# Three attention stages and two feed-forward stages of a transformer kernel merged into one sequence of 24 batches with a guest in the slots

## What is computed

```python
x = x + L0_attn(layernorm(x))   # block mask: 16 heads of 8, scores outside the allowed blocks are 0, biases
x = x + L0_ffn(layernorm(x))    # FP4: (silu(xq @ Wg) * (xq @ Wu)) quantised again, @ Wd; hidden 352
x = x + L1_attn(layernorm(x))   # causal mask with ALiBi bias
x = x + L1_ffn(layernorm(x))    # ternary: silu(w1) * w2, then two square 512x512 layers with gelu, w3
x = x + L2_attn(layernorm(x))   # full softmax, no output projection
x = x + L2_ffn(layernorm(x))    # RWKV
x = x + L3_attn(layernorm(x))   # state-space block
x = x + L3_ffn(layernorm(x))    # eight low-rank experts
```

## Time and profile before

| what | value |
|---|---|
| median of three runs | 2219.01 us (2218.09 to 2221.08) |
| profiled execution, span from first to last instruction | 2215.5 us |
| instructions | 34423 |
| busy PE, DVE, ACT, POOL | 1867.7, 1282.6, 1049.3, 712.8 us |
| mean granted TensorE clock | 0.921 |

### The profile page before, as it was taken

The page is one execution under the profiler, slowest core; times in us unless marked ns, Lnnn a source line. Parts: engine busy times, 40 slices in busy tenths (PEclk is TensorE's granted clock), DMA queues, the critical chain, the costliest instruction groups (busy, mean ns, idle before and its releaser), DMA issues.

```text
span 2215.5 us, 34423 instructions
## 1 busy us (share of the span) xinstructions
PE 1867.7 (84%) x12909; PEld 864.2 (39%) x12909; DVE 1282.6 (58%) x2930; ACT 1049.3 (47%) x1768; POOL 712.8 (32%) x796
## 2 busy tenths in 40 slices
PE   2788788756569989998999999899999967999998
PEld 0233233224344555554444444333333324444443
DVE  1666666637767666673110111489989916776663
ACT  1266565532123655565222222188888854445432
POOL 3176666545532322220110011122233115443330
PEclk9799999867868999998899999799999978999999
DMA  8323343000023343220000002143223110000000
GB/s 195 66 58 67 71 87 65 1 11 1 1 57 59 68 89 77 59 59 2 2 0 1 0 1 57 26 89 60 59 58 81 36 48 1 1 10 5 6 5 15
DMA packets 70270, 91.58 MB, mean 41 GB/s; under 512 B 13228, under 2 KB 63772, under 8 KB 65228
## 3 DMA queue, kind: packets, MB, share of 16 engines
q1 hardware_dynamic: 64536, 84.42, 18.5%
q10 hardware_dynamic: 5568, 4.96, 0.7%
HBM read 49.10 MB, written 39.85 MB: 40 GB/s over the span
## 4 chain that ended last, share of the span: by engine, by line
PE 52%; issue 5%; DVE 5%; ACT 4%; DMA 2%; SPq 1%; POOL 1%; DVEq 0%; POOLq 0%; ACTq 0%
PE ps L1401 9%; PE ps L417 5%; DVE mx L685 3%; PE ps L2798 3%; PE ps L391 3%; PE ps L375 3%; PE ps L2078 2%; PE ps L403 2%; PE ps L2080 2%; PE ps L2096 2%; PE ps L353 2%; PE ps L330 2%; PE ps L1391 2%; DMA Qst<-mT 1%; PE ps L1771 1%
## 5 line engine op out<-in xcount | busy, mean ns | idle before, releaser
L685 DVE TENSOR_REDUCE mx<-ps 128x1 f32<-128x512 f32 (+3 forms) x1536 | 755.8, 549 | 255.8 <-PE ps L353 121.4
L593 ACT ACTIVATE Pr<-ps 128x1024 f32<-128x1024 f32 (+3 forms) x512 | 350.1, 705 | 233.0 <-PE ps L335 117.4
L586 ACT ACTIVATE Pr<-ps 128x512 f32<-128x512 f32 x512 | 274.6, 600 | 48.4 <-PE ps L391 43.1
L353 PE MATMUL ps<-Kst,Qst 63*128 63x512 bf16 (+3 forms) x1024 | 235.2, 326 | 60.8 <-DVE mx L685 38.2
L330 PE MATMUL ps<-Qst,Kst 64*128 64x512 bf16 (+3 forms) x1024 | 229.2, 324 | 48.6 <-issue 32.1
L375 PE MATMUL ps<-Pr,V 128*32 128x512 f32 (+3 forms) x2048 | 204.5, 473 | 4.4 <-ACT ctxU L599 3.1
L403 PE MATMUL ps<-Kst,Qst 63*128 63x512 bf16 x512 | 169.3, 401 | 6.6 <-DVE mx L685 4.4
L417 PE MATMUL ps<-Pr,V 128*32 128x256 f32 x2048 | 165.1, 394 | 8.4 <-ACT ctxU L599 7.5
L2826 POOL TENSOR_TENSOR ve<-mv,eps 128x4 f32<-128x4 f32 x41 | 8.8, 214 | 502.4 <-DVE mv L2815 502.4
L391 PE MATMUL ps<-Qst,Kst 64*128 64x512 bf16 x512 | 154.4, 388 | 14.9 <-issue 9.0
L1509 DVE SCALAR_TENSOR_TENSOR f_shared<-ps,w_L_s_w,f_own 128x512 f32<-128x512 f32 x32 | 23.4, 748 | 230.6 <-ACT f_own L1462 199.6
(11 more groups left out here) (342 smaller groups left out, 3355.5 us busy)
## 6 DMA issues: line engine op xcount, KB each, us to landing
Qst<-parts_scratch SPq DMA_DIRECT2D x48, 384.0 KB, 6.0
Kst<-parts_scratch SPq DMA_DIRECT2D x48, 384.0 KB, 8.4
parts_scratch<-qpart SPq DMA_DIRECT2D x48, 192.0 KB, 2.7
parts_scratch<-kpart SPq DMA_DIRECT2D x48, 192.0 KB, 2.7
parts_scratch<-qpart SPq DMA_DIRECT2D x48, 128.0 KB, 2.6
parts_scratch<-kpart SPq DMA_DIRECT2D x48, 128.0 KB, 2.7
parts_scratch<-qpart SPq DMA_DIRECT2D x48, 64.0 KB, 2.3
parts_scratch<-kpart SPq DMA_DIRECT2D x48, 64.0 KB, 2.3
```

Of the source, the lines that this page charges most:

```text
L353: mm = pe.matmul(ps[:, 4 + a, lo:lo + W], k.Qst[rows, n.par, pair, P * it:P * it + P], k.Kst[rows, n.par, pair, 0:W], start=True, stop=not ...
L586: act.activation(k.Pr[:, g % 2, 2 * (j // 2) + 1 - j % 2, :], ps[:, self.bank_t(b, g, j), :], ACT.Exp).then_inc(self.s_exp.sem, 1)
L593: act.activation(k.Pr[:, g % 2, 2 * tile:2 * tile + 2, 0:W], ps[:, 2 * tile:2 * tile + 2, 0:W], ACT.Exp).then_inc(self.s_exp.sem, 1)
L685: dve.tensor_reduce(k.mx[:, half, at:at + 1], ps[:, bank, lo:lo + W], AX_X, ALU.max, negate=True).then_inc(self.s_max.sem, 1)
```

## The change

The stages `Attention`, `Fp4Ffn`, `Attention`, `TernaryFfn`, `Attention` become one object `Run` with 26 frames (numbers -1 to 24), whose frame F holds batch F of a sequence of 24: eight of the block, eight of the alibi, eight of the full attention. There is no wait for a whole stage any more until the tail. A feed-forward is a guest of the frames: `Fp4Ffn` in frames 2 to 10 (its first half for batch F-2, its second half for batch F-3), `TernaryFfn` in frames 11 to 19 (the same, with F-11 and F-12). Its matmuls stand in three places of a slot, between the attention's own. From frame 20 on there is no guest.

PSUM is divided anew: banks 0 and 1 transposed scores, 2 and 3 scores for the maxima, 4 and 5 guest, 6 context, 7 the rest. So a tile of transposed scores has one pair of banks where it had two. The two heads of a tile are issued next to each other, and one DVE reduction reads both heads. In the full attention each kind takes turns in two banks up to frame 19 and in three from frame 20.

The guest's own work changes: ACT's silu and gelu read and write SBUF in one instruction over all columns (1408 for FP4, 2048 for ternary), after DVE (ternary) or ACT (FP4) has copied the products out of PSUM; each needs a table load before it and one after it for the exponentials. The square layers are computed bank by bank. The block attention's power of minus one on POOL becomes a reciprocal on DVE (`dve_recip`). The norm of a guest has tiles of its own.

```diff
-        frames(pe, frame)
...
+class Run:
+    FRAMES = range(-1, 3 * NB + 1)
+    LONE = 20
...
+    def guests(self, F):
+        fp4, ternary = self.ffns
+        out = []
+        if F <= NB + 2:
+            out.append(fp4)
+        if F >= ternary.FIRST - 1:
+            out.append(ternary)
+        return out
...
+    def pe_quarter(self, pe, F, s, part, b, g, pb, pg, mb, c):
+        hosting = F < self.LONE
+        t, tn = self.of(b)
+        if t:
+            if t.kind == "full":
+                t.pe_head_t(pe, tn, g, part, hosting)
+            elif part % 2 == 0:
+                t.pe_scores_t(pe, tn, g, part // 2)
+        if part in (0, 2):
+            self.pe_guest(pe, F, s, part)
+        m, mn = self.of(mb)
+        if m:
+            if m.kind == "full":
+                m.pe_head_m(pe, mn, c, part, hosting)
+            elif part % 2 == 0:
+                m.pe_scores_m(pe, mn, c, part // 2)
+        p, pn = self.of(pb)
+        if p and p.kind == "full" and part % 2:
+            p.pe_context(pe, pn, pg, part // 2, 2)
+        elif p and p.kind != "full" and part == 3:
+            p.pe_context(pe, pn, pg, 0, 1)
+        if part == 1:
+            self.pe_guest(pe, F, s, part)
+            self.pe_out(pe, F, s)
...
+    def act_exps(self, act, F, s, b, g):
...
+            t.act_exps(act, tn, g, 0)
+        self.act_guest(act, F, s, 0)
+        if t:
+            t.act_exps(act, tn, g, 1)
...
-            out = ps[:, 2 * tile + a, 0:W]
...
+    def pe_scores_t(self, pe, b, g, tile):
+        pe.wait_ge(self.s_exp.sem, self.s_exp.at(b, 2 * g + tile))
...
+        for a in (1, 0):
+            rows = slice(64 * a, 64 * a + 64)
+            mm = pe.matmul(ps[:, PAIR_T + a, 0:W], k.Kst[rows, b.par, 2 * q + tile, P * jt:P * jt + P],
+                           k.Qst[rows, b.par, 2 * q + tile, T - W:T], start=True, stop=not tri)
...
-                    dve.tensor_reduce(k.mx[:, half, at:at + 1], ps[:, bank, lo:lo + W], AX_X,
+            dve.tensor_reduce(heads[:, :, 4 * i + it:4 * i + it + 1], k.ps[:, PAIR_M:PAIR_M + 2, lo:lo + W], AX_X,
+                              ALU.max, negate=True).then_inc(self.s_max.sem, 2)
...
+    def bank_t(self, b, g, j, hosting):
+        t = 64 * b.c + 4 * g + j
+        return PAIR_T + t % 2 if hosting else t % 3
...
-            pool.tensor_tensor(k.rec[:, :, :], k.dn2[:, :, :],
-                               k.mone[:, 0:1].unsqueeze(2).broadcast_to([P, NT, 4]), ALU.pow)                .then_inc(self.s_part.sem, 1)
+        dve.reciprocal(k.rec[:, :, :], k.dn2[:, :, :]).then_inc(self.s_recip.sem, 1)
...
-class TernaryFfn(Stage):
+class TernaryFfn(Ffn):
+    UNITS = ((("turn",), ("h2", 0, 0), ("h2", 0, 1)),
+             (("h2", 0, 2), ("h2", 0, 3), ("gate", 0)),
...
+    FIRST = 11
+    SILU, GELU_B, GELU_A = 3, 9, 14
...
-                act.activation(dst[:, m, :], ps[:, src + m, :], ACT.Gelu, scale=scale[:, m:m + 1])\
-                   .then_inc(done.sem, 1)
+            act.activation(self.h, self.h, ACT.Silu).then_inc(self.s_gate.sem, 1)
...
+            act.activation(self.a, self.a, ACT.Gelu).then_inc(self.s_a.sem, 1)
...
+    def dve_first(self, dve, n, j):
+        dve.tensor_scalar(self.a[:, j, :], self.k.ps[:, self.bank(self.H1 + j), :], self.sh1[:, j:j + 1], None,
+                          ALU.mult).then_inc(self.s_a_raw.sem, 1)
```

More of the change, by code:

```diff
@@ L45, in valid @@
     def valid(self):
[L46 to L51 removed]
+        return 0 <= self.c < NB
 class Signal:
@@ new lines, in pe_scores_m @@
+    def pe_scores_m(self, pe, n, c, r):
+        k, ps = self.k, self.k.ps
+        pair, rounds = self.rounds(c)
+        if r >= len(rounds):
+            return
+        u, its = rounds[r]
+        if u == 0:
+            pe.wait_ge(self.s_stacked.sem, self.s_stacked.at(n))
+        pe.wait_ge(self.s_max.sem, self.s_max.at(n, u))
+        tri = self.kind == "alibi"
+        for it in its:
+            W, lo = self.span(it), self.place(its, it)
+            for a in range(2):
+                rows = slice(64 * a, 64 * a + MROW)
+                mm = pe.matmul(ps[:, PAIR_M + a, lo:lo + W], k.Qst[rows, n.par, pair, P * it:P * it + P],
+                               k.Kst[rows, n.par, pair, 0:W], start=True, stop=not tri)
+            if tri:
+                for part in range(2):
+                    for a in range(2):
+                        end = slice(64 * a, 64 * a + 64)
+                        mm = pe.matmul(ps[:, PAIR_M + a, lo + W - P:lo + W], k.ident_h[end, part, :],
+                                       k.tri_qk[end, part, :], start=False, stop=part == 1)
+        mm.then_inc(self.s_scores.sem, 2 * len(its))
@@ L1441, in tensor, with pe_alone @@
-        ahead(pe, frame)
+        k.first_start(pe)
+        for F in self.FRAMES:
+            if F == 0:
+                pe.wait_ge(k.s_weights, 16 * len(k.loads))
+            if F == self.LONE:
+                self.pe_alone(pe)
+            for s, (b, g), (pb, pg), (mb, c) in slots(F):
+                for part in range(4):
+                    self.pe_quarter(pe, F, s, part, b, g, pb, pg, mb, c)
+                self.pe_misc(pe, F, s)
+    def pe_alone(self, pe):
+        full, n = self.full, N(self.LONE - 2 * NB)
+        pe.wait_ge(full.s_exp.sem, full.s_exp.at(n.plus(-1), 4 * 8))
+        pe.wait_ge(full.s_max.sem, full.s_max.at(n, 8))
+        done = self.ffns[1].s_out
+        pe.wait_ge(done.sem, done.at(N(NB - 1)))
@@ L2921, in _ @@
                .then_inc(k.s_prepared, 1)
-            for st in stages:
-                st.scalar(act)
+            run.scalar(act)
+            tail.scalar(act)
         @block.vector
@@ L2935, in _ @@
                 pe.sem_inc(sig.sem, sig.start)
-            for st in stages:
-                st.tensor(pe)
+            run.tensor(pe)
+            tail.tensor(pe)
 def kernel(**inputs):
```

2473 lines of the change are left out of this document (1205 added, 1268 removed), and 11 rows, old and new, of the table UNITS.

## The result

Changed kernel: **2268.48 us** (median of 4 runs), kernel before beside it 2219.86 (4 runs); ratio 1.0228, 95% interval 1.0204 to 1.0252. One of the four runs of the changed kernel, at a mean granted clock of 0.556, took 3047.03 us and is left out of the ratio; the other three lie between 2266.32 and 2268.57. I had forecast 1992 (1900 to 2130) and given "slower" 7%. The profiled execution took 2266.32 us with a span of 2264.4.

The account below looks back on a forecast made before the run. Each stage had its own limit: PE in ternary, DVE in full, round trips in block and FP4; seams between stages held 122 us. Frame sums 155 + 488 + 731 + 184 + 21 + 409 = 1988, plus 3.5: 1992 us (1900 to 2130).

Parts of the forecast that it names:

- The base of the block frame: Block attention frame without a guest: 47.3 us, by the pace of the last writes of x.
- a chain of 38 us: Block frames: one pair of banks makes PE and ACT alternate, exponential plus 0.5 us, 32 times 1.2 us.
- FP4's price: Block frames hosting FP4: 55 us taken, between 47.3 all hidden and 66.6 nothing hidden.
- Frames -1 to 1: First frames, without a guest: frame 1 ends near 153, 2 us for FP4 weights, 155 us.
- Alibi and ternary: Alibi frames hosting ternary: PE full, 36 + 44.5 = 80.5 us, with 3% for waits 83.
- Full and ternary: Full attention frames hosting ternary: PE's 35 + 6.5 + 44.5 = 86 us, with waits 91.
- the broken pairs: Full frames: a guest between two paired score products breaks the pair, twice a slot in 15 slots, 6.5 us.
- the single places: Ternary as guest: matmuls in some 29 separate places a frame cost 0.19 us more each, 5.6 us.
- Long activations: Ternary frames: three long ACT steps of 4.5 us stop exponentials; the table loads cost the span about 8 us.
- DVE and POOL: Busy times: DVE about the same (maxima 77 us less, reciprocals 8 and copies 72 more), POOL 93 us less.
- Plain addition: Rival: hosts and guests share nothing, frames of 66.6 and 65 with FP4, 89 with ternary; 2110 us, 23%.
- The slower rival: Single pair of banks ties PE to ACT, long steps stop the kernel, 139 us over plain addition; 2250 us, 7%.

Follow-up runs that it names:

- e1: Changed kernel with the whole work of both guests left out, banks, order and waits kept: 1829.5 us.
- e17: e1 with the guest's banks for the second tile of transposed scores, maxima of one head each, and the context product early: 1665.7 us.
- e13: FP4's quantiser rounds only a quarter, against a kernel with context early, guest banks lent and guest grouped in full frames: 2156.9 us.
- e6: Changed kernel with the guests' silu and gelu as plain copies of the same size, so no table switches in the frames: 2212.5 us.
- e5: Changed kernel with the context product of block and alibi attention moved earlier, behind the first maxima's scores: 2230.2 us.
- e9: Changed kernel with the guest of quarters 0 and 2 behind both score products of the full attention: 2259.8 us.
- e10: e9 with the guest's units of a slot put in one place in the full attention's frames: 2245.4 us.
- all mends: Changed kernel with context early, guest banks lent, guest regrouped in full and alibi frames, and FP4's down projection in halves: 2186.39 us, ratio 0.9864 to the kernel before.

## Why the prediction was wrong

- **The base of the block frame.** "No engine is full at 47", and a chain of 38 us "on top of which come those copies and table loads". This step failed first, and it is the largest: 10.2 of the 17.7 us that a block frame with FP4 took over the forecast. It took 47.3 as what a frame costs without a guest; it costs 57.5 (e1). The chain counted an exponential and 0.5 us per tile, 32 times, and put all of PE's other work beside it. In PE's list nearly all of that work stands behind the second tile. I had the order of the list and the pair of banks before me and summed only one of the two alternations. That order and banks are the cause is shown: with both changed the frame takes 47.9 (e17).
- **FP4's price.** 55 - 47.3 = 7.7 forecast, 15.2 measured, 18.8 on the better order. I had said that DVE's long steps stand together and let that count for little. In e13 and e6 each microsecond taken from DVE or ACT shortened the frame by about one or more, part of it by way of POOL and the clock. In this ring of round trips an engine's idle time wasn't room.
- **Frames -1 to 1.** 155 forecast, 188.6 measured, the same cause: next to nothing is hosted there, but the order and the one pair hold there too (e5: 173.7). e17, with no guest and both mends, starts frame 2 at 164.2; the 9 us that are left stay open.
- **Alibi and ternary.** 83 against 90.4. That PE is full was right (busy 349 of 362 us at a clock of 0.99), and so was the guest's price: by the starts of neighbouring matmuls ternary takes 45.9 us of the frame (44.5 forecast). What failed is the attention's own sum: it takes 44.5 us with its waits where I had 36 and 2.5. The context products alone take 11.8 instead of 8.6 (11.3 in the kernel before, by its starts). How much of the other 5 us is waiting isn't known; PE is idle only (361.70 - 348.75)/4 = 3.2 us a frame by the modelled ends. Without a guest the frame takes 57.7, so ternary costs 32.7 of its 43: here hosting hides 10.3 us, but the slower host takes 11.7 (57.7 against 46).
- **Full and ternary.** 91 against 97.7. The mechanism was right in kind, the broken pairs and the single places: I had 6.5 and 5.6 us for them, and e9 and e10 give back 3.6 and 4.3. The term that failed is the 35 us for the frame. The half slot of 1.10 us holds score products and context, and none of the transposes and projections that stand between half slots. I left them at nothing here, though I had counted them for alibi. One such step, in the kernel before:

```profile
1557.05 0.66 PE L2798 MATMUL ps<-ident,ctxU 128*128 128x128 f32 x4
1557.64 0.39 PE L391 MATMUL ps<-Qst,Kst 64*128 64x512 bf16 x1
```

  0.59 us to the next start, and all of them take 6.6 us a frame there. In frames 17 and 18, by starts, the guest takes 45.6 us, the scores 25.4, the context 18.6, and transposes and projections 8.0, together 97.6: without the last it is 89.6, and my sum with its waits was 91. With two banks of each kind the frame takes 51.4 us even without a guest (e1), which I hadn't priced either.
- **Long activations.** I had some 8 us for the span; their table loads alone cost 56 (in e6 activations of the same size stay in), 5 of 15 us in every FP4 frame, where I counted two loads but no stop (the clock has its part in e6's gain). The row on the table load held: silu starts 1.30 us after its load here as in the earlier trace rows, exponentials too (449.74 to 451.04). The further drain that the Trainium skill (ScalarE: Activation LUTs, What ACT_TABLE_LOAD costs) states doesn't show here either; the loss lies in the loads themselves and in what waits behind them.
- **DVE and POOL.** DVE's busy time rose by 43.6 us where I had about 3: the maxima went from 755.8 to 408.5 + 320.8 = 729.3 us, 26.5 less and not 77. POOL fell by 56, not 93: the 93.0 of L827 went, but its splits of q and k (L793 before, L536 now) take 217 us instead of 185, in groups of 23 instead of 21 and with means up to 1392 ns where 1159 was the longest.
- **The rivals.** Plain addition had the right picture and too cheap hosts (66.6, 89). The slower rival named 80 us as the mean of the 18 hosting frames from which it decides, and they took (650.3 + 809.9)/18 = 81.1; but its mechanism was mostly wrong: 56 us from the long activations' table loads, where it had 139 from the whole steps. So that it named the right pace is luck in part. The rest lies in the slower host and in DVE's work for FP4. Right were the tail, the full frames alone and the seams. These are gone, but the slower frames took back their 122 us and 49 more.

Still open: alibi frames with ternary stay at 87 us even with all mends, and how much of that is waiting wasn't tried. The clock of 0.86 in the block frames can't be set in a run, so its share of the 10 us of the host and of the 15 us of FP4 is unknown.

## What to carry to other kernels

Price the host without its guest first: if merging changes its banks or the order of its list, that price is paid in every frame, and here it ate the seams. Before idle time of an engine is counted as room for a guest, see whether that engine is idle because it waits in a ring; here the guest's work then added nearly whole. In an ordered queue, put its own work evenly beside each of the waits that it has.
